# The values of both query halves of a key tile in every second step, in two 512-key attentions

## The chip, the cores and the metric

One core of a Trainium2 chip runs the whole kernel as one launch. The metric is the device time in microseconds (us), the median over runs.

## The reference

The kernel computes a two-layer decoder for 4 sequences of 512 tokens with 128 channels, in fp32. Six blocks follow one another, each added to the residual stream behind a layer norm: an RWKV recurrence, a cross attention to 32 context rows, a feed-forward block that holds a causal attention and a mixture of experts, an attention with relative positions, a latent cross attention, and an attention whose keys are split in two classes. The change concerns the two attentions over 512 keys with 16 heads of 8 channels. Cut to what matters:

```python
# causal, in the feed-forward block ("da" in the kernel)
scores = jnp.einsum('bqhd,bkhd->bhqk', q, k) / np.sqrt(hd)
scores = jnp.where(causal, scores, jnp.finfo(scores.dtype).min)
attn = jax.nn.softmax(scores, axis=-1)
o = jnp.einsum('bhqk,bkhd->bqhd', attn, v).reshape(b, s, d)

# with classes of keys, in the last block ("ga" in the kernel)
l = jnp.where(key_mask[:, None, None, :], logits, -jnp.inf)
a = jax.nn.softmax(l, axis=-1)
return jnp.einsum('bhqk,bkhd->bqhd', a, v)
```

## The kernel before

The blocks run one after the other. Both attentions are built by one function, `attention_stage` (line 508), called as "da" at line 904 (causal) and as "ga" at line 2006 (with classes). Channels lie on partitions. The stage first projects q, k and v and splits q and k into bf16 parts. Then come 16 units, one for each of 4 sequences and 4 groups of four heads (`QUADS`), of eight steps each: 128 steps (`STEPS`). A step covers two heads (`pr`) and one of four tiles of 128 queries or keys.

Each engine has its own instruction queue, whose order is written out by hand; semaphores join them. TensorE's loop (line 742) has 144 iterations. In iteration `step` it issues, in this order:

- `scores(step)` (line 673, matmuls at line 682): queries by keys for two heads, in two of four PSUM banks. VectorE reduces them to row maxima (line 844). A ring of two groups of banks is shared with the turn of the maxima, so that scores wait for what used the slot two places before.
- `scores_t(t)` (line 707, matmuls at 717) with t = step - 13: the transposed scores, keys by queries, less the maxima, in three PSUM banks. They wait until the first of the two exponentials of step t - 1 is done (`exped`). ScalarE turns them into exponentials (`exponentials`, line 783), which lie in three slots of key tiles (`pt`).
- in da only, `mask_scores(step)` (line 693), which adds the causal mask to the scores.
- in every eighth iteration `turn_maxima` (line 702), behind the four small operations of `split_maxima` on VectorE (lines 832 to 838). ScalarE copies the result (line 791), and a DMA puts it beside the queries.
- `values(p)` (line 722, matmuls at 736) with p = step - 16: the exponentials of one key tile times the values, for one half of the queries (`half`), four heads in four column groups of TensorE, added up in one PSUM bank. They wait for the exponentials of the key tile, in da for GpSimd's masking of them (line 643), and at a unit's first for ScalarE's copy of the last unit's output (line 796, `o_out`).

Where the mask leaves a half no queries (`half_of`), `values` does nothing: in da key tiles 2 and 3 have only the second half, and key tile 1 has 128 columns of the first.

Of the kernel before, what the change touches and what calls it, by code (L numbers as in the profile page):

```python
# [504 lines left out]
STEPS = 8 * QUADS  # L505


def attention_stage(nc, g, tag, xn, wq, wk, wv, group, scale, o, causal=False, classes=None):
# [5 lines left out]
    S_LAG, V_LAG = 13, 3  # L514
# [7 lines left out]
    def half_of(kt, half):  # L522
        return max(first_query(kt), half * (T // 2)), (half + 1) * (T // 2)
# [9 lines left out]
    for step in range(STEPS + S_LAG):  # L533
        if step < STEPS:
            ring.append(("scores", step + 1))
        if step % 8 == 1 and 8 < step < STEPS + 8:
            turn_slot[step // 8 - 1] = len(ring)
            ring.append(("maxima", step // 8))
    score_bank = [2 * (n % S_GROUPS) for n, (what, _) in enumerate(ring) if what == "scores"]
    score_slot = [n for n, (what, _) in enumerate(ring) if what == "scores"]  # L540

    with ExitStack() as ctx:
# [9 lines left out]
        with ExitStack() as inner:  # L552
# [21 lines left out]
            with nc.Block() as block:  # L574
# [72 lines left out]
                def _(pe):  # L647
# [25 lines left out]
                    def scores(step):  # L673
                        u, r = divmod(step, 8)
                        pr, qt = divmod(r, 4)
                        if r == 0:
                            pe.wait_ge(stack_loaded[u % NBUF], 16 * LOADS * (u // NBUF + 1))
                        wait_ring(score_slot[step])
                        keys = keys_of(qt)
                        for par in range(2):  # L680
                            rows = slice(64 * par, 64 * par + KS)
                            last = nc.tensor.matmul(g.ps[:, score_bank[step] + par, 0:keys],  # L682
                                                    qst[rows, u % NBUF, pr, bass.ts(qt, 128)],
                                                    kst[rows, u % NBUF, pr, 0:keys], start=True, stop=not causal)
                        if not causal:
                            last.then_inc(scored, 1)

                    def mask_scores(step):
                        qt = step % 4
                        for par in range(2):  # L690
                            bank = score_bank[step] + par
                            for j in range(4):
                                last = nc.tensor.matmul(g.ps[32 * j:32 * j + 32, bank, bass.ts(qt, 128)],  # L693
                                                        g.ident_bf[:, bass.ts(j, 32)], g.lowered_bf[:, :],
                                                        start=False, stop=True)
                        last.then_inc(scored, 1)

                    def turn_maxima(u):
                        pe.wait_ge(split4, u + 1)
                        wait_ring(turn_slot[u])  # L700
                        for qt in range(QT):
                            last = nc.tensor.matmul(g.ps[0:12, 2 * (turn_slot[u] % S_GROUPS), bass.ts(qt, 128)],
                                                    mparts[:, u % 2, qt, :, :, :].rearrange("p a n r -> p (a n r)"),
                                                    g.ident_bf[:, :], start=True, stop=True)
                        last.then_inc(m_turned, 1)

                    def scores_t(t):
                        u, r = divmod(t, 8)
                        kt, pr = divmod(r, 2)
                        if r == 0:  # L710
                            pe.wait_ge(m_loaded[u % 2], 32 * (u // 2 + 1))
                        if t >= 1:
                            pe.wait_ge(exped, 2 * t - 1)
                        q0 = first_query(kt)
                        for par in range(2):
                            rows = slice(64 * par, 64 * par + KT)
                            last = nc.tensor.matmul(g.ps[:, ST_BANK + (2 * t + par) % ST_BANKS, q0:T],  # L717
                                                    kst[rows, u % NBUF, pr, bass.ts(kt, 128)],
                                                    qst[rows, u % NBUF, pr, q0:T], start=True, stop=True)
                        last.then_inc(st_scored, 1)  # L720

                    def values(p):
                        u, r = divmod(p, 8)
                        kt, half = divmod(r, 2)
                        b, quad = divmod(u, 4)
                        lo, hi = half_of(kt, half)
                        if lo >= hi:
                            return
                        if causal:
                            pe.wait_ge(selected, 8 * u + 2 * kt + 2)  # L730
                        else:
                            pe.wait_ge(exped, 2 * (8 * u + 2 * kt + 2))
                        if r == 0 and u >= 1:
                            pe.wait_ge(o_out, u)
                        for j in range(4):
                            last = nc.tensor.matmul(g.ps[32 * j:32 * j + HD + 1, O_BANK, lo:hi],  # L736
                                                    v9[:, QT * b + kt, 4 * quad + j, :],
                                                    pt[:, (4 * u + kt) % SLOTS, j, lo:hi],
                                                    start=r == 0, stop=kt == QT - 1, skip_group_check=True)
                        last.then_inc(pv_done, 1)  # L740

                    for step in range(STEPS + S_LAG + V_LAG):
                        t = step - S_LAG
                        if step < STEPS:
                            scores(step)
                        if 0 <= t < STEPS:
                            scores_t(t)
                        if causal and step < STEPS:
                            mask_scores(step)
                        if step % 8 == 1 and step // 8 - 1 in turn_slot:  # L750
                            turn_maxima(step // 8 - 1)
                        if 0 <= t - V_LAG < STEPS:
                            values(t - V_LAG)

                @block.scalar
                def _(act):
# [1397 lines left out]
```

## Time and profile before

| | us |
|---|---|
| median of 3 runs | 1505.38 (1504.9 to 1508.01) |
| the profiled execution: its time | 1507.97 |
| its span, first to last instruction | 1506.0 |
| TensorE (PE) busy | 1160.2 (77%) |
| VectorE (DVE) busy | 844.8 (56%) |
| ScalarE (ACT) busy | 707.9 (47%) |
| GpSimd (POOL) busy | 306.2 (20%) |
| mean granted TensorE clock | 0.903 of full speed |

Busy times are those of one profiled execution, added up over stages with different limits; each stage has to be read by itself. da's steps lie between about 240 and 403 us of the span, ga's between about 1288 and 1474 us. A row of the timeline gives the start and the length of a run of like instructions; PE rows are matmuls, whose ends are modelled, so that starts tell more than ends. An fp32 matmul stands in the trace as two instructions.

### The profile page before, as it was taken

The numbers are of one execution on the slowest core, as the hardware profiler recorded it, in microseconds if no ns is written. First come the engines' busy times: TensorE is split into PE (matmuls) and PEld (weight loads), VectorE is DVE, ScalarE is ACT, GpSimd is POOL, SyncE is SP. The second block draws the span as 40 slices with busy tenths as digits, with TensorE's granted clock in tenths as the row PEclk, the third lists the DMA queues.
The fourth block names the chain that finished last, engine by engine and source line by source line (L and its number), as shares of the span: only waits on it lengthen the run. The fifth ranks groups of instructions, "written<-read, shape, count | busy, mean of one in ns | idle before, by whom it ended". The sixth has DMA issues, their size and how long they took to land. (4 is left out here: it accounts for less than half of the span.)

```text
span 1506.0 us, 35692 instructions
## 1 busy us (share of the span) xinstructions
PE 1160.2 (77%) x14780; PEld 580.4 (39%) x14780; DVE 844.8 (56%) x1358; ACT 707.9 (47%) x1322; POOL 306.2 (20%) x639
## 2 busy tenths in 40 slices
PE   5677686888748997568999999999666647588884
PEld 2222332333223442246666666666342224122221
DVE  3575336777552223246666666666146234799965
ACT  4101443777522223535565565655232313389891
POOL 1443020333202322033233232222002002000000
PEclk9999866999968999789999999999789878599998
DMA  4000005111005320240030030200200001411100
GB/s 160 1 0 0 1 31 180 47 50 40 2 0 114 68 45 0 73 69 3 4 24 3 5 22 4 15 6 3 15 1 0 1 1 61 156 41 43 38 14 28
DMA packets 133665, 51.61 MB, mean 34 GB/s; under 512 B 103113, under 2 KB 125657, under 8 KB 132858
## 3 DMA queue, kind: packets, MB, share of 16 engines
q1 hardware_dynamic: 133506, 49.34, 14.1%
q8 instruction: 118, 1.93, 0.6%
q14 instruction: 41, 0.34, 0.1%
HBM read 33.12 MB, written 15.81 MB: 32 GB/s over the span
## 5 line engine op out<-in xcount | busy, mean ns | idle before, releaser
L1714 DVE TENSOR_REDUCE re_nmax<-ps 128x1 f32<-128x512 f32 x256 | 158.9, 682 | 113.5 <-PE ps L1548 113.5
L1563 PE MATMUL ps<-const,re_p 128*128 128x128 f32 x1024 | 154.9, 284 | 32.9 <-DVE re_pT L1729 27.0
L1681 ACT ACTIVATE re_p<-ps,re_nmax 128x512 f32<-128x512 f32 x256 | 154.5, 693 | 16.7 <-DVE re_nmax L1714 16.7
L844 DVE TENSOR_REDUCE ga_nmax<-ps 128x2 f32<-128x1024 f32 x128 | 147.7, 1216 | 9.1 <-PE ps L682 9.1
L1670 ACT ACTIVATE re_pT<-ps 128x512 f32<-128x512 f32 x128 | 76.6, 598 | 161.7 <-PE ps L1563 161.7
L783 ACT ACTIVATE ga_pt<-ps 128x512 f32<-128x512 f32 x256 | 139.2, 598 | 20.4 <-PE ps L717 18.6
L1563 PEld LDWEIGHTS ps<-const,re_p 128*128 128x128 f32 x1024 | 109.2, 142 | 63.4 <-ACT re_p L1681 47.1
L844 DVE TENSOR_REDUCE da_nmax<-ps 128x2 f32<-128x256 f32 (+3 forms) x128 | 102.6, 822 | 33.5 <-PE ps L693 32.0
L783 ACT ACTIVATE da_pt<-ps 128x512 f32<-128x512 f32 (+3 forms) x256 | 97.5, 438 | 38.5 <-PE ps L717 37.3
L1729 DVE COPY re_pT<-ps 128x512 f32<-128x512 f32 x128 | 82.5, 685 | 23.2 <-PE ps L1563 22.5
L736 PE MATMUL ps<-ga_pt,ga_v 128*9 128x256 f32 x1024 | 81.4, 386 | 10.3 <-ACT ga_osum L796 10.1
L1069 DVE TENSOR_TENSOR ex_u<-ps,ex_s 128x512 f32<-128x512 f32 x48 | 33.1, 690 | 95.9 <-PE ps L1042 95.9
L163 ACT ACT_TABLE_LOAD x8 | 10.3, 1283 | 152.2 <-PEq L298 92.0
L1538 PE MATMUL ps<-re_keys,re_qbd 32*128 32x512 f32 x512 | 74.8, 655 | 5.5 <-POOL re_qbd L1502 5.5
L643 POOL TENSOR_SCALAR_AFFINE_SELECT da_pt<-da_pt 128x256 f32<-128x256 f32 x128 | 52.7, 412 | 125.4 <-ACT da_pt L783 125.2
L1055 ACT ACTIVATE ex_s<-ps 128x512 f32<-128x512 f32 x48 | 28.7, 597 | 92.8 <-PE ps L1042 92.8
L1511 POOL TENSOR_TENSOR re_qrel<-re_qd,const 128x64 f32<-128x64 f32 x256 | 68.6, 301 | 4.8 <-DMA re_qd<-re_q_scratch 4.8
L1082 POOL TENSOR_TENSOR ex_u<-ex_u,ex_gates 128x512 f32<-128x512 f32 x32 | 40.4, 1264 | 142.7 <-DMA ex_gates<-gates_scratch 73.5
L682 PE MATMUL ps<-ga_kst,ga_qst 50*128 50x512 bf16 x256 | 53.7, 419 | 19.7 <-ACT ga_v L769 10.2
L1498 POOL TENSOR_TENSOR re_keys<-re_k,vec 128x64 f32<-128x64 f32 (+1 forms) x60 | 17.3, 289 | 249.5 <-PE ps L1548 249.5
L1613 PE MATMUL ps<-re_pT,re_v_far 128*9 128x128 f32 x1536 | 65.2, 285 | 0.5 <-ACT re_osum L1690 0.5
L736 PE MATMUL ps<-da_pt,da_v 128*9 128x256 f32 (+1 forms) x768 | 56.2, 362 | 6.3 <-ACT da_osum L796 6.3
(379 smaller groups left out, 2028.6 us busy)
## 6 DMA issues: line engine op xcount, KB each, us to landing
ex_gates<-gates_scratch SPq DMA_DIRECT2D x4, 2048.0 KB, 15.3
da_stacks<-da_qkparts SPq DMA_DIRECT2D x8, 384.0 KB, 3.1
da_qst<-da_stacks SPq DMA_DIRECT2D x32, 96.0 KB, 2.3
da_kst<-da_stacks SPq DMA_DIRECT2D x32, 96.0 KB, 2.3
ga_stacks<-ga_qkparts SPq DMA_DIRECT2D x8, 384.0 KB, 3.1
ga_qst<-ga_stacks SPq DMA_DIRECT2D x32, 96.0 KB
ga_kst<-ga_stacks SPq DMA_DIRECT2D x32, 96.0 KB
da_stacks<-da_qkparts SPq DMA_DIRECT2D x8, 256.0 KB, 3.1
```

Source lines behind the costliest of these rows:

```text
L682: last = nc.tensor.matmul(g.ps[:, score_bank[step] + par, 0:keys], qst[rows, u % NBUF, pr, bass.ts(qt, 128)], kst[rows, u % NBUF, pr, 0:ke ...
L736: last = nc.tensor.matmul(g.ps[32 * j:32 * j + HD + 1, O_BANK, lo:hi], v9[:, QT * b + kt, 4 * quad + j, :], pt[:, (4 * u + kt) % SLOTS, j, ...
L783: nc.scalar.activation(pt[:, (4 * u + kt) % SLOTS, 2 * pr + par, q0:T], g.ps[:, ST_BANK + (2 * t + par) % ST_BANKS, q0:T], ACT.Exp)\
L844: nc.vector.tensor_reduce(nmax[:, u % 2, :, pr, qt], g.ps[:, score_bank[step]:score_bank[step] + 2, 0:keys_of(qt)], AX.X, ALU.max, negate= ...
L1511: nc.gpsimd.tensor_tensor(qrel[:, m, pair, :, :, :, two], qd[:, b % 2, OCT * at:OCT * at + OCT, 4 * pair:4 * pair + 4].unsqueeze(2) .broad ...
L1538: nc.tensor.matmul(g.ps[:, S_BANK + quad, :], qbd[rows, m, :, :, :].rearrange("p o h c -> p (o h c)"), keys[rows, b % 2, m, :], start=True ...
L1563: last = nc.tensor.transpose(g.ps[:, T_BANK + tile % 2, bass.ts(kt, 128)], p[:, QUAD_ORDER[idx], bass.ts(kt, 128)], g.c("ident"))
L1613: last = nc.tensor.matmul(g.ps[32 * j:32 * j + HD + 1, V_BANK, bass.ts(quad, 128)], values, weights, start=kt == 0, stop=kt == QT - 1)
L1670: nc.scalar.activation(pT_of(s, QUAD_ORDER[idx]), turned_of(4 * s + idx), ACT.Identity)\
L1681: nc.scalar.activation(p[:, quad, :], g.ps[:, S_BANK + quad, :], ACT.Exp, bias=nmax[:, s % 2, idx:idx + 1]).then_inc(exped, 1)
L1714: nc.vector.tensor_reduce(nmax[:, s % 2, idx:idx + 1], g.ps[:, S_BANK + quad, :], AX.X, ALU.max, negate=True).then_inc(maxed, 1)
L1729: nc.vector.tensor_copy(pT_of(s, QUAD_ORDER[idx]), turned_of(4 * s + idx))\
```

## The change

Until now `values(p)` came in every iteration from 16 on, one half of the queries each. Now an iteration with an even p issues none, and one with an odd p issues the even half first and then its own. Both belong to the same key tile. The arithmetic stays as it is.

```diff
--- before.py
+++ after.py
@@ -749,8 +749,10 @@
                             mask_scores(step)
                         if step % 8 == 1 and step // 8 - 1 in turn_slot:
                             turn_maxima(step // 8 - 1)
-                        if 0 <= t - V_LAG < STEPS:
-                            values(t - V_LAG)
+                        p = t - V_LAG
+                        if 0 <= p < STEPS and p % 2 == 1:
+                            values(p - 1)
+                            values(p)
 
                 @block.scalar
                 def _(act):
```

## Rows read from the trace of the kernel before

**Rows 1.** Page, costliest groups: busy us, mean ns, idle before, releaser; VectorE's maxima.

```profile
L844 DVE TENSOR_REDUCE ga_nmax<-ps 128x2 f32<-128x1024 f32 x128 | 147.7, 1216 | 9.1 <-PE ps L682 9.1
...
L844 DVE TENSOR_REDUCE da_nmax<-ps 128x2 f32<-128x256 f32 (+3 forms) x128 | 102.6, 822 | 33.5 <-PE ps L693 32.0
```

**Rows 2.** Busy by engine: us; PE, PEld, DVE, ACT, POOL; clock; DMA share; GB/s.

```profile
1311.00:1463.00 152.00, 132.83 (x1436) 37.00 (x1427) 137.26 (x167) 137.21 (x261) 0.00 (x0) 0.99 0.12 35
260.00:390.00 130.00, 112.19 (x2063) 44.48 (x2062) 98.76 (x166) 98.44 (x253) 46.17 (x112) 0.99 0.14 40
```

**Rows 3.** Timeline of PE, ga: start, us, line, tiles, count; one ordinary step.

```profile
1388.69 0.39 PE L682 MATMUL ps<-ga_kst,ga_qst 50*128 50x512 bf16 x2
1388.91 0.38 PE L717 MATMUL ps<-ga_qst,ga_kst 53*128 53x512 bf16 x2
1389.23 0.62 PE L736 MATMUL ps<-ga_pt,ga_v 128*9 128x256 f32 x8
1389.78 0.39 PE L682 MATMUL ps<-ga_kst,ga_qst 50*128 50x512 bf16 x2
```

**Rows 4.** Timeline of ga, all engines: start of one unit and the turn.

```profile
1320.57 0.62 PE L736 MATMUL ps<-ga_pt,ga_v 128*9 128x256 f32 x8 [0.67 <-ACT ga_osum L796]
...
1382.05 1.21 DVE L844 TENSOR_REDUCE ga_nmax<-ps 128x2 f32<-128x1024 f32 x1
...
1383.85 0.62 PE L736 MATMUL ps<-ga_pt,ga_v 128*9 128x256 f32 x8 [0.67 <-ACT ga_osum L796]
...
1384.10 2.35 DVE L844 TENSOR_REDUCE ga_nmax<-ps 128x2 f32<-128x1024 f32 x2
...
1384.63 0.38 PE L717 MATMUL ps<-ga_qst,ga_kst 53*128 53x512 bf16 x2
1385.06 1.09 ACT L783 ACTIVATE ga_pt<-ps 128x512 f32<-128x512 f32 x2 [0.36 <-PE ps L717]
...
1385.47 0.33 PE L702 MATMUL ps<-identb,ga_mparts 128*12 128x128 bf16 x3 [0.45 <-DVE ga_nmax L844]
...
1386.51 0.39 PE L682 MATMUL ps<-ga_kst,ga_qst 50*128 50x512 bf16 x2 [0.23 <-DVE ga_nmax L844]
...
1386.94 6.88 DVE L844 TENSOR_REDUCE ga_nmax<-ps 128x2 f32<-128x1024 f32 x6 [0.49 <-PE ps L682]
```

**Rows 5.** Timeline of PE, tail of ga, where no scores are left.

```profile
1468.98 0.39 PE L717 MATMUL ps<-ga_qst,ga_kst 53*128 53x512 bf16 x2
1469.30 0.62 PE L736 MATMUL ps<-ga_pt,ga_v 128*9 128x256 f32 x8
1470.07 0.39 PE L717 MATMUL ps<-ga_qst,ga_kst 53*128 53x512 bf16 x2
...
1471.47 1.05 PE L736 MATMUL ps<-ga_pt,ga_v 128*9 128x256 f32 x16
```

**Rows 6.** Timeline of da, all engines: one unit from its first values.

```profile
332.43 0.62 PE L736 MATMUL ps<-da_pt,da_v 128*9 128x256 f32 x8 [0.40 <-ACT da_osum L796]
...
333.22 1.13 DVE L844 TENSOR_REDUCE da_nmax<-ps 128x2 f32<-128x256 f32 x2
...
333.79 0.33 PE L702 MATMUL ps<-identb,da_mparts 128*12 128x128 bf16 x3 [0.18 <-DVE da_nmax L844]
...
334.53 0.34 PE L682 MATMUL ps<-da_kst,da_qst 48*128 48x384 bf16 x2
...
335.26 2.42 DVE L844 TENSOR_REDUCE da_nmax<-ps 128x2 f32<-128x768 f32 x3 [0.91 <-PE ps L693]
...
337.41 0.28 PE L682 MATMUL ps<-da_kst,da_qst 48*128 48x256 bf16 x2 [0.50 <-DVE da_nmax L844]
```

**Rows 7.** Timeline of PE at the start of ga, at the lower clock.

```profile
1308.58 1.04 PE L736 MATMUL ps<-ga_pt,ga_v 128*9 128x256 f32 x8
...
1309.55 0.61 PE L682 MATMUL ps<-ga_kst,ga_qst 50*128 50x512 bf16 x2
```

**Rows 8.** Busy by engine, in the relative attention.

```profile
780.00:1080.00 300.00, 265.34 (x6694) 183.96 (x6694) 185.06 (x363) 166.98 (x288) 79.15 (x258) 0.99 0.13 10
```

## The prediction, made before the changed kernel was run

> **What bounds the kernel now.** I read the page first, for which of its groups belong to the two 512-key attentions ("da", the causal one, and "ga", the one with classes), then each stage by itself, then one unit of eight steps in order of time. The page's two groups for line 844 show that VectorE spends 147.7 us on the row maxima in ga with 9.1 us idle before them, and 102.6 us in da with 33.5 us idle, all of it until TensorE delivered [rows 1]. Over a steady stretch of ga, VectorE is busy for 137.26 of 152 us, ScalarE for 137.21 and TensorE for 132.83, all at a granted clock of 0.99; in da TensorE leads with 112.19 of 130 us [rows 2]. So no engine of ga has more than a tenth to spare, and what counts is the order on TensorE's queue.
>
> One ordinary step of ga on that queue is scores, then transposed scores (0.22 us later), then values (0.32 us), then the next scores (0.55 us): 1.09 us from one step's scores to the next one's [rows 3]. VectorE's six reduces in a row take 6.88 us, the last of them 1.22 us, which is a pitch of 1.13 us [rows 4]; this and not TensorE's 1.09 us paces the middle of a unit. Once in a unit VectorE is late for another reason. After the last reduce of a unit come the four small splits, so the next reduce starts 2.05 us after that last one (1382.05 to 1384.10). The turn of the maxima can start only 1.37 us later (1385.47), since it waits for that reduce; the scores behind the turn wait for the next reduce (idle 0.23 us, until 1386.51), and VectorE sits idle for 0.49 us until 1386.94 [rows 4]. The other gap, 0.67 us in which TensorE waits for line 796's copy of the output at 1383.85, delays no reduce: VectorE is at its splits then [rows 4]. From that wait at 1320.57 to the same one at 1383.85 are six units: 10.55 us each [rows 4].
>
> A third chain is hidden just under this one. The transposed scores of a step wait for the first exponential of the step before. In the tail of ga, where no scores are left, transposed scores follow one another at 1468.98 and 1470.07 although the values between them, started at 1469.30, need only 0.55 us of the queue: 1.09 us is the round from transposed scores over ScalarE back to transposed scores [rows 5, 3]. ScalarE starts 0.43 us after they start (1384.63 to 1385.06) [rows 4]. It holds no second step in store, so every delay of transposed scores over 1.09 us is idle time of ScalarE.
>
> **The change part by part.** Nothing is added or removed but the order: the four (eight in the trace, each in two passes) matmuls of an even step p go one iteration later, directly ahead of those of p + 1. Only TensorE's queue changes; no DMA and nothing of SP or POOL moves. The waits move with the matmuls and both halves wait for the same exponentials, which are in by then. The slot of the exponentials comes free with the odd half, whose iteration stays. The wait for line 796's copy goes one iteration later and vanishes. I cost this removal at nothing: it hid under the splits (above). If that cover were not there it would be worth 0.67 us a unit in ga and 0.40 us in da [rows 4, 6].
>
> *The double block.* The tail of ga shows exactly this arrangement: two steps' values one behind the other are 1.05 us from first start to last end, one step's are 0.62 us [rows 5]. The second block costs 0.43 us. So the double block holds the queue for 0.55 + 0.43 = 0.98 us, where two single ones took 1.10. This is less because a block by itself also pays the change of the array's shape: 0.55 is 0.43 and 0.12 more. The Trainium skill, TensorEngine Tiling (Array Packing), section Key Properties, says that a change of tiling mode drains TensorE; the rows agree with the direction, and this rule alone speaks for the change (rival below).
>
> *ga, an ordinary pair.* Put the transposed scores of the long iteration (odd step) at 0. Values start at 0.32, the next scores at 0.32 + 0.98 = 1.30, the short iteration's transposed scores at 1.52. They come 0.43 us too late for ScalarE (1.52 against the round of 1.09). The next long iteration's transposed scores need the short one's first exponential, so they come at 1.52 + 1.09 = 2.61. VectorE needs 2 x 1.13 = 2.26 for the pair and is no longer the bound.
>
> *ga, the pair with the turn.* VectorE can start on the short iteration's scores at 1.30 + 0.43 = 1.73 (the 0.43 from 1386.51 to 1386.94, [rows 4]), on the long one's 1.13 later, at 2.86, which is 0.25 after the long transposed scores at 2.61. At the end of a unit the next unit's first reduce is 2.05 behind that, at 2.30 after those; and the following long iteration starts at 2.61, so this reduce starts at -0.31 of it. The turn comes 1.37 after, at 1.06. From the turn to the next scores TensorE by itself needs 0.74 us with one block of this size (da: 333.79 to 334.53, [rows 6]), so 1.17 with two: scores at 2.23, transposed scores at 2.45, the next long iteration at 2.45 + 1.09 = 3.54.
>
> A unit of ga is then 3 x 2.61 + 3.54 = 11.37 us against 10.55: 0.82 us more. Steps 16 to 127 are 14 such units: 11.5 us. In the tail, 13 steps without scores, a pair takes 0.32 + 0.98 + 1.09 = 2.39 against 2 x 1.09: 0.21 us, six times, 1.3 us. Together 12.8 us.
>
> *da.* With the causal mask only the first two key tiles have queries in the first half, so only two of eight blocks move: the 256-column one of key tile 0, into the iteration with the turn, and a 128-column one of key tile 1. The iteration that the first one leaves has time for it anyway: the turn at 333.79 still waits for the reduce pair that begins at 333.22 behind the splits [rows 6]. The one it joins has none: turn, values, scores at 334.53, then the mask, and VectorE, idle for 0.91 us, starts its reduce at 335.26 [rows 6]. All this comes 0.43 us later. Its three reduces from there run without a gap in 2.42 us, and at 337.41 the scores wait 0.50 us for them, so the shift is handed on to the next unit and no slack takes it up [rows 6]. The 128-column block moves to where those 0.50 us absorb its 0.21 us. So 0.43 x 14 = 6.0 us.
>
> Sum: 12.8 + 6.0 = 18.8 us. The profiled execution has a span of 1506.0 us and took 1507.97, 2.6 us above the median of 1505.38; it would become a span of 1524.8 and a run of 1526.8, and the median 1524.2. I say **1524 us**, 1.2% slower.
>
> **Bounds of the unknown.** The step that no row shows is a double block with scores behind it. Its upper end is two full blocks, 1.10: 0.12 more in four pairs a unit of ga and once a unit in da, 14 x 0.60 = 8.4 us, 1533. The lower end is that ga's pairs are hidden (VectorE's 2.26 us still rules) and da alone pays: 1505.4 + 6.0 = 1511. I take 0.43, since its row has the same two blocks.
>
> **Rivals.**
> *Hidden after all.* ScalarE's 9% of idle time in ga [rows 2] is where slack could come from, if its second exponential and the next step's first could be moved together. Against it stands that the round of 1.09 us goes through the first exponential alone. If it holds for ga only: 1511 us. If da's shift is also taken up (a gap among those three reduces would do it): 1505 us.
> *Faster.* TensorE's queue is the real bound, and each pair saves a change of shape in and one out: 0.12 us behind the values and 0.32 - 0.22 = 0.10 ahead of them, 0.22 us. It decides if the short iteration's transposed scores can come at most 2.26 - 1.09 = 1.17 us after the long one's; they come at 1.52. 56 pairs and the freed waits of 0.67 us would be more than VectorE's whole idle time of 9.1 us, which caps the gain [rows 1]: 1496 us. The skill's rule of the drain, by itself, would give this sign; for it is the busy share of TensorE.
> *The clock.* The double block leaves TensorE idle for some 0.65 us in each pair (2.61 less the 1.96 of queue time). If the granted clock fell to the lower level, as at the start of ga, where the way from values to scores takes 0.97 us and not 0.55 [rows 7], TensorE's part of the pair (2.61 less the 0.66 of 1.09 - 0.43 that is ScalarE's) would become 1.95 x 0.97 / 0.55 = 3.44, and the pair 4.10 us. That is 1.5 us more a pair, 6 us a unit; three such units make 1542 us. Against it: in the relative attention from 780 to 1080 us TensorE was busy for 265.34 of 300 us, with idle time of its own, at a granted clock of 0.99 [rows 8]. For it: the share here falls to about 0.8.
> That the program would not do what it says has no chance worth a line: each engine's order is written out by hand.
>
> **How the numbers follow.** Forecast of 1524 us: 0.81. Clock, about 1542: 0.06. Only da pays, 1511: 0.05. All hidden, 1505: 0.05. Faster, 1496: 0.03. Within 0.2% is about what a measurement of this kernel can tell from no change. Slower by more than that: 0.81 + 0.06 + 0.05 = 0.92; same 0.05; faster 0.03. The range of 1511 to 1535 takes in both bounds and the da-only case and leaves out the clock, the hidden and the faster case, 0.14, and some chance that a term is further off.
>
> **What would show it.** In ga's timeline after: 16 values matmuls in a row over some 1.05 us; transposed scores that alternate between 1.52 and 1.09 us apart; ScalarE idle about 0.4 us once in two steps with TensorE's line 717 as the releaser; VectorE's idle time before line 844 up from 9.1 to over 20 us; a unit of 11.4 us. The wait for the output copy is gone in both stages. In da the reduce behind the turn waits 1.3 us in place of 0.91 and a unit grows by 0.43 us. Wrong would be: pairs of 2.26 us in ga (the third chain is misread), a second block of 0.55 us, or a granted clock well under 0.98 in ga.

## The result: slower by 2.1%, more than forecast

| | us |
|---|---|
| changed kernel, median of 6 runs | 1539.49 (1536.33 to 1548.22) |
| kernel before, median of 6 runs | 1507.61 (1504.9 to 1516.85) |
| ratio | 1.021 (95% interval 1.018 to 1.024) |
| profiled execution after: time, span | 1539.57, 1537.8 |
| forecast | 1524 (1511 to 1535) |

The sign was right. The size was not: 31.8 us more span against a forecast of 18.8. The page's costliest groups after, with busy us, mean ns, idle before and releaser, answer to [rows 1]:

```profile
L846 DVE TENSOR_REDUCE ga_nmax<-ps 128x2 f32<-128x1024 f32 x128 | 150.3, 1219 | 19.5 <-PE ps L682 19.5
L785 ACT ACTIVATE ga_pt<-ps 128x512 f32<-128x512 f32 x256 | 138.8, 595 | 31.8 <-PE ps L717 30.5
...
L846 DVE TENSOR_REDUCE da_nmax<-ps 128x2 f32<-128x256 f32 (+3 forms) x128 | 101.2, 821 | 49.1 <-PE ps L693 47.9
...
L717 PE MATMUL ps<-ga_qst,ga_kst 53*128 53x512 bf16 x256 | 50.6, 391 | 32.7 <-ACT ga_pt L785 32.7
```

VectorE's idle time in ga went from 9.1 to 19.5 us and in da from 33.5 to 49.1, and TensorE now stands for 32.7 us ahead of ga's transposed scores, released by ScalarE. The most useful measure in this document is the length of a unit, from one copy of the output on ScalarE (line 796 before, 798 after) to the next:

| kernel | da: first to last copy, us | ga: first to last copy, us | ordinary unit of da | of ga |
|---|---|---|---|---|
| before | 135.46 | 154.02 | 9.20 | 10.55 |
| changed | 150.31 | 166.64 | 9.63, and six of 11.0 to 11.2 | 11.47 |

The two differences, 14.9 and 12.6, are 27.5 of the 31.8 us. The double blocks begin in a stage's first unit, ahead of its first copy. Counted from a stage's first reduce (239.30 and 1288.26 us before, 240.18 and 1306.59 after) to its last copy, da grew by 15.2 us and ga by 13.7, together 28.9. Of the other 2.9 us, 0.9 come ahead of da's first reduce (it starts anywhere from 236.9 to 242.5 us in the experiments below) and 2.2 between da's last copy and ga's first reduce (885.5 us before, 887.8 after, 885.6 to 894.9 in the experiments, in no order that follows their edits); the end is 0.2 us shorter. These 2.9 us I count as not explained by the change.

In ga TensorE's timeline is what the prediction drew (start, us, line, tiles, count, idle before and releaser). It starts in the iteration with the turn and answers to [rows 3, 4]:

```profile
1363.34 0.39 PE L717 MATMUL ps<-ga_qst,ga_kst 53*128 53x512 bf16 x2 [0.48 <-ACT ga_pt L785]
1364.42 0.33 PE L702 MATMUL ps<-identb,ga_mparts 128*12 128x128 bf16 x3 [0.69 <-DVE ga_nmax L846]
...
1365.60 0.39 PE L682 MATMUL ps<-ga_kst,ga_qst 50*128 50x512 bf16 x2
1365.82 0.38 PE L717 MATMUL ps<-ga_qst,ga_kst 53*128 53x512 bf16 x2
...
1366.90 0.39 PE L717 MATMUL ps<-ga_qst,ga_kst 53*128 53x512 bf16 x2 [0.47 <-ACT ga_pt L785]
1367.22 1.05 PE L736 MATMUL ps<-ga_pt,ga_v 128*9 128x256 f32 x16
1368.20 0.39 PE L682 MATMUL ps<-ga_kst,ga_qst 50*128 50x512 bf16 x2
1368.43 0.38 PE L717 MATMUL ps<-ga_qst,ga_kst 53*128 53x512 bf16 x2
1368.65 0.38 PE L682 MATMUL ps<-ga_kst,ga_qst 50*128 50x512 bf16 x2
1369.59 0.39 PE L717 MATMUL ps<-ga_qst,ga_kst 53*128 53x512 bf16 x2 [0.56 <-ACT ga_pt L785]
1369.91 1.05 PE L736 MATMUL ps<-ga_pt,ga_v 128*9 128x256 f32 x16
...
1372.20 0.39 PE L717 MATMUL ps<-ga_qst,ga_kst 53*128 53x512 bf16 x2 [0.48 <-ACT ga_pt L785]
```

The double block holds the queue from 1367.22 to 1368.20, 0.98 us. The ordinary pair from 1369.59 to 1372.20, from one long iteration's transposed scores to the next one's, is 2.61 us, the pair with the turn 3.56 (forecast 3.54). Only the pair from 1366.90 is off, 2.69 us.

In da, what the prediction had not placed there is seen in the busy time by engine of two neighbouring units (length; PE, PEld, DVE, ACT, POOL; granted clock; DMA share; GB/s), and at their turns:

```profile
309.89:319.52 9.63, 8.12 (x150) 3.57 (x148) 7.00 (x13) 7.03 (x19) 3.31 (x8) 1.00 0.16 44
319.52:330.49 10.97, 9.44 (x150) 4.04 (x148) 7.01 (x13) 7.04 (x20) 3.30 (x8) 0.84 0.13 38
```

```profile
310.65 0.28 PE L682 MATMUL ps<-da_kst,da_qst 48*128 48x256 bf16 x2 [0.41 <-DVE da_nmax L846]
...
312.00 0.33 PE L702 MATMUL ps<-identb,da_mparts 128*12 128x128 bf16 x3 [0.55 <-DVE da_nmax L846]
...
312.22 1.03 PE L736 MATMUL ps<-da_pt,da_v 128*9 128x256 f32 x13
...
320.29 0.28 PE L682 MATMUL ps<-da_kst,da_qst 48*128 48x256 bf16 x2 [0.41 <-DVE da_nmax L846]
...
321.62 0.48 PE L702 MATMUL ps<-identb,da_mparts 128*12 128x128 bf16 x3 [0.55 <-DVE da_nmax L846]
...
322.00 1.91 PE L736 MATMUL ps<-da_pt,da_v 128*9 128x256 f32 x13
```

Both units do the same work. In the first the clock stays at its upper level, and the unit takes 9.63 us. In the second the mean granted clock is 0.84: 0.16 of 10.97 us, twice since the lower level is half of the upper, are some 3.5 us at the lower level. It shows from the turn on, where the same 13 matmuls take 1.91 us in place of 1.03. Read in windows of 0.2 us, each of the changed kernel's six falls in da begins between 0.60 us before the turn and 0.05 us after it.

### The profile page after: what moved, and what is told of

Its sections match the earlier page's. It is cut to its first block and busy times, and to the rows that moved or that the text cites. A ratio compares the mean times of both kernels' runs of the same rounds, so it can differ in the third digit from the quotient of the medians.

```text
span 1537.8 us, 35692 instructions
## 1 busy us (share of the span) xinstructions
PE 1164.6 (76%) x14780; PEld 595.9 (39%) x14780; DVE 846.7 (55%) x1358; ACT 710.2 (46%) x1322; POOL 306.2 (20%) x639
## 5 line engine op out<-in xcount | busy, mean ns | idle before, releaser
L846 DVE TENSOR_REDUCE ga_nmax<-ps 128x2 f32<-128x1024 f32 x128 | 150.3, 1219 | 19.5 <-PE ps L682 19.5
L785 ACT ACTIVATE ga_pt<-ps 128x512 f32<-128x512 f32 x256 | 138.8, 595 | 31.8 <-PE ps L717 30.5
L846 DVE TENSOR_REDUCE da_nmax<-ps 128x2 f32<-128x256 f32 (+3 forms) x128 | 101.2, 821 | 49.1 <-PE ps L693 47.9
L717 PE MATMUL ps<-ga_qst,ga_kst 53*128 53x512 bf16 x256 | 50.6, 391 | 32.7 <-ACT ga_pt L785 32.7
L736 PE MATMUL ps<-ga_pt,ga_v 128*9 128x256 f32 x1024 | 69.2, 384 | 0.2 <-ACT ga_pt L785 0.2
## 6 DMA issues: line engine op xcount, KB each, us to landing
ex_gates<-gates_scratch SPq DMA_DIRECT2D x4, 2048.0 KB, 14.9
```

Source lines behind the costliest of these rows:

```text
L785: nc.scalar.activation(pt[:, (4 * u + kt) % SLOTS, 2 * pr + par, q0:T], g.ps[:, ST_BANK + (2 * t + par) % ST_BANKS, q0:T], ACT.Exp)\
L846: nc.vector.tensor_reduce(nmax[:, u % 2, :, pr, qt], g.ps[:, score_bank[step]:score_bank[step] + 2, 0:keys_of(qt)], AX.X, ALU.max, negate= ...
```

## The experiments

All edits are in `attention_stage`. Two theories are told apart for each stage. For ga, **theory A**: each pair waits for the round from transposed scores over the first exponential back; **rival B**: the load of an engine over the pair counts. For the clock in da, **theory I**: it falls because the moved block leaves TensorE's queue thin ahead of the turn; **theory D**: it falls because of the dense double block behind it. In the expectations of the first four runs "Theory A" stands for what the timelines above say of the stage at hand.

### Each stage alone

```diff
-                        if 0 <= t - V_LAG < STEPS:
-                            values(t - V_LAG)
+                        p = t - V_LAG
+                        late = lambda n: n % 2 == 0 and not causal
+                        if 0 <= p < STEPS:
+                            if p % 2 == 1 and late(p - 1):
+                                values(p - 1)
+                            if not late(p):
+                                values(p)
```

> The change in ga alone; da as before. Theory A (each stage pays by itself, and ga's cost is the round from transposed scores over ScalarE, cut by the double block): ga grows by what it grew in the changed kernel, some 14 us, units of 11.47 us and not 10.55, and the granted clock in ga stays at 1.00; ratio about 1.009. Rival (a stage's time depends on what the earlier one leaves, or ga's growth was partly the clock's phase): ga grows by another amount, under 10 or over 18 us.

Measured: 1526.42 us, ratio 1.0116 (1.0077 to 1.0156). ga's units are 11.47 us, first to last copy 166.64 us as in the changed kernel; da is 135.73 us. So each stage pays by itself, and ga's cost is 12.6 us between its copies (13.7 from its first reduce on).

The same edit with `n % 2 == 0 and causal`:

> The change in da alone; ga as before. Theory A: da grows by some 15 us, of which 5.6 to 6 us are the block that comes 0.43 us later in each unit, and 8 to 9 us are units of 11.0 us in which the granted clock falls to its lower level behind the turn; units of 9.63 us between them; ratio about 1.010. Rival (the fall of the clock was a chance of that run): all units are 9.63 us, da grows by 6 us, ratio 1.004.

Measured: 1527.71 us, ratio 1.0113 (1.0079 to 1.0148). ga is 154.03 us, as before. da is 152.52 us, 17.1 more than before, with units of 9.63 us and seven of 11.0 to 11.3. The fall of the clock was no chance of one run.

### Each of da's two blocks alone

With `n % 8 == 2 and causal` only the 128-column block of key tile 1 moves:

> In da only the 128-column block of key tile 1 (p = 2 in each unit) goes behind, into the iteration of p = 3; key tile 0 and ga stay. Theory A: it joins where VectorE is late anyway, so a unit stays at 9.20 us, the granted clock at 0.99 and the time within 0.1%. Rival (any double block costs its own length, or makes the clock fall): 0.2 us a unit, 3 us, or units of 11 us.

Measured: 1513.78 us, ratio 1.003 (1.0006 to 1.0053). A unit of da is 9.20 us, as forecast, save four of 9.45 to 9.47 (the kernel before has one such) and the last two (9.14 and 7.50 where the kernel before has 8.73 and 6.87); none is near 11 us. da is 137.32 us, 1.9 more than before, but the block itself costs nothing in an ordinary unit. The rest of the 0.3% lies outside the two stages (922.4 us between them against 917.1), where nothing was edited. "Within 0.1%" was a miss for the whole kernel.

With `n % 8 == 0 and causal` only the 256-column block of key tile 0 moves:

> In da only the 256-column block of key tile 0 (p = 0) goes behind, into the iteration with the turn. Theory A: this block alone makes both parts of da's cost: units of 9.63 us where the clock stays, 11.0 us where it falls, da 15 us longer, ratio about 1.010. Rival (both blocks share in it): da grows by clearly less than in the kernel with both, 8 us or so.

Measured: 1526.64 us, ratio 1.0101 (1.0066 to 1.0135); da 148.89 us, units of 9.63 and five of 11.0 to 11.2 us. This block alone makes both parts of da's cost.

### Is it the empty queue or the double block?

The first answer keeps the double blocks and fills the queue where the moved block was:

```diff
-                            for j in range(4):
+                            for n in range(16 if step % 8 == 0 else 4):
+                                j = n % 4
                                 last = nc.tensor.matmul(g.ps[32 * j:32 * j + 32, bank, bass.ts(qt, 128)],
                                                         g.ident_bf[:, bass.ts(j, 32)], g.lowered_bf[:, :],
-                                                        start=False, stop=True)
+                                                        start=False, stop=n >= (12 if step % 8 == 0 else 0))
```

> As the run with the change in da alone, but the mask's eight matmuls of every unit's first step are issued four times (the mask is added again where it already forbids, so the result is the same). They fill some 0.3 of the 0.4 us in which TensorE now waits there for VectorE, the place where the moved block used to be. Theory I (the clock falls because the queue has run thin ahead of the turn): it stays at its upper level, all units are about 9.63 us, da is 8 us shorter than in the run without the filling, ratio 1.005 or so. Theory D (it falls because of the dense double block behind the turn): the falls stay, with units of 11 us in every second place, ratio 1.011.

Measured: 1518.34 us, ratio 1.005 (1.0022 to 1.0077). Two of its units and the stretch from 271 us on, by engine:

```profile
280.24:289.87 9.63, 8.46 (x174) 3.90 (x172) 7.02 (x13) 7.04 (x20) 3.30 (x8) 1.00 0.17 46
289.87:299.50 9.63, 8.46 (x174) 3.91 (x172) 7.01 (x13) 7.03 (x20) 3.30 (x8) 1.00 0.15 44
271.00:400.00 129.00, 112.03 (x2248) 51.41 (x2235) 92.56 (x161) 93.64 (x240) 43.94 (x107) 0.99 0.13 37
```

The same stretch with the change in da alone:

```profile
271.00:400.00 129.00, 110.23 (x1867) 47.18 (x1862) 87.29 (x149) 87.40 (x226) 41.13 (x100) 0.92 0.13 37
```

TensorE does more matmuls, and of the first thirteen units twelve are 9.63 us and one 9.89. Only the next to last is long, 11.31, at a mean granted clock of 0.57; no scores are left there, so there is no mask to repeat. da is 144.35 us in place of 152.52. More work on TensorE made the stage 8.2 us shorter. With the queue filled the double blocks do no harm to the clock in these thirteen units. The filling closes the wait in the unit's first step; the one of 0.55 us ahead of the turn stays:

```profile
299.55 0.63 PE L694 MATMUL ps<-loweredb,identb 128*32 128x128 bf16 x32
300.26 0.28 PE L682 MATMUL ps<-da_kst,da_qst 48*128 48x256 bf16 x2
...
301.60 0.33 PE L703 MATMUL ps<-identb,da_mparts 128*12 128x128 bf16 x3 [0.55 <-DVE da_nmax L850]
```

The second answer takes the moved block away altogether, so that the queue is thin and nothing is joined. This kernel is the one before, and it leaves a part of the causal attention's output out. In da only:

```diff
-        return lo < hi
+        return lo < hi and not (causal and p % 8 == 0)
...
-                        if lo >= hi:
+                        if not has_queries(p):
                             return
...
-                        if r == 0 and u >= 1:
+                        if r == (1 if causal else 0) and u >= 1:
                             pe.wait_ge(o_out, u)
```

> The kernel before with the 256-column values block of key tile 0, first half, left out of da (that part of the causal attention's output is missing). Nothing is joined anywhere; TensorE's queue in the unit's first step is as empty as in the changed kernel. Theory I: the granted clock falls behind the turn in some or every second unit, which makes those units 0.5 to 1.4 us longer than 9.20 although there is less work. Theory D: no double block, so the clock stays at 1.00 and every unit is 9.20 us; no slower than before.

Measured: 1518.65 us, ratio 1.0053 (1.0028 to 1.0077). The first two units:

```profile
267.18:277.69 10.51, 8.94 (x142) 3.40 (x140) 7.11 (x13) 7.04 (x20) 3.31 (x8) 0.84 0.14 41
277.69:286.88 9.19, 7.58 (x142) 3.10 (x140) 7.01 (x13) 7.03 (x19) 3.30 (x8) 1.00 0.17 47
```

Five units are 10.5 to 10.6 us, the others 9.2; da is 141.97 us. Leaving work out made the stage 6.5 us longer than before. The waits ahead of the scores and the turn are 0.41 and 0.55 us again. Theory D is out: the clock falls in a kernel without double blocks and holds in one that has them. Theory I fits both runs. What they do not separate is where in the unit TensorE's work is missing from how much of it is missing. Each clean unit of a kernel without falls keeps TensorE busy for more of its time (7.97 of 9.20 us before, 8.46 of 9.63 filled) than those of the kernels with falls (8.12 of 9.63 changed, 7.58 of 9.20 with the block out). That the falls begin at the turn speaks for the place; the same filling put elsewhere in the unit was not run.

### Which part of ScalarE's work holds ga

Both runs are the one with the change in ga alone, with one of the two exponentials of each step cut to half its columns:

```diff
                         for par in range(2):
+                            end = T // 2 if par == 0 and not causal else T
-                            nc.scalar.activation(pt[:, (4 * u + kt) % SLOTS, 2 * pr + par, q0:T],
+                            nc.scalar.activation(pt[:, (4 * u + kt) % SLOTS, 2 * pr + par, q0:end],
```

> As the run with the change in ga alone, but the first of each step's two exponentials in ga covers 256 of the 512 columns (part of the attention's output is not computed). Theory A (the round from transposed scores over the first exponential back): the round shrinks from 1.09 by about 0.25 us, a unit from 11.47 to about 10.5, where VectorE is the bound again. Rival B (ScalarE's or TensorE's whole load of a pair counts): as much with the second exponential shortened as with the first.

With `par == 1`:

> The counterpart: the second of each step's two exponentials in ga covers 256 of the 512 columns. ScalarE has the same work as in the run with the first one shortened. Theory A: the second exponential lies outside the round, so a unit stays within 0.1 us of 11.47. Rival B: a unit of about 10.5 us as with the first.

Measured: 1516.42 us, ratio 1.0038 (1.0011 to 1.0065), with the first one cut; 1523.93 us, 1.009 (1.0059 to 1.0121), with the second. Transposed scores in TensorE's timeline with the first cut:

```profile
1350.70 0.39 PE L719 MATMUL ps<-ga_qst,ga_kst 53*128 53x512 bf16 x2 [0.33 <-ACT ga_pt L791]
1351.02 1.05 PE L738 MATMUL ps<-ga_pt,ga_v 128*9 128x256 f32 x16
...
1353.09 0.39 PE L719 MATMUL ps<-ga_qst,ga_kst 53*128 53x512 bf16 x2 [0.26 <-ACT ga_pt L791]
```

And with the second cut:

```profile
1354.02 0.39 PE L719 MATMUL ps<-ga_qst,ga_kst 53*128 53x512 bf16 x2 [0.48 <-ACT ga_pt L791]
1354.34 1.05 PE L738 MATMUL ps<-ga_pt,ga_v 128*9 128x256 f32 x16
...
1356.62 0.39 PE L719 MATMUL ps<-ga_qst,ga_kst 53*128 53x512 bf16 x2 [0.48 <-ACT ga_pt L791]
```

The pair is 2.39 us in the first and 2.60 in the second, as long as with both whole. The units are 11.04 and 11.47 us. ScalarE has the same work in both (the slots are set to ones once, at the stage's start, in both), so its load is not the cause; the round through the first exponential is. My number for the unit, 10.5, was a miss: three pairs shrank by 0.21 to 0.22 us each, but the pair with the turn grew from 3.56 to 3.78. There TensorE now waits 1.12 us for VectorE's reduce, and behind the turn the double block still keeps VectorE idle for 0.63 us.

### The order around the turn

In the changed kernel, and in the kernel before, the values are issued ahead of the turn:

```diff
-                        if step % 8 == 1 and step // 8 - 1 in turn_slot:
-                            turn_maxima(step // 8 - 1)
...
+                        if step % 8 == 1 and step // 8 - 1 in turn_slot:
+                            turn_maxima(step // 8 - 1)
```

> The changed kernel, but in the iteration that has both, the double block of values goes ahead of the turn of the maxima and not behind it. Theory I with the sums of the prediction: in da the double block then fills the time in which the queue waits for VectorE anyway, so the block no longer delays the scores (unit back to 9.2 us or a little less), the queue is not empty ahead of the turn, and the granted clock does not fall: da loses its whole 15 us. In ga the three ordinary pairs of 2.61 us stay, so the unit stays between 11.3 and 11.5 us: ratio to the kernel before about 1.009. Rival (the double block itself brings the clock down, or costs its length wherever it stands): da stays 6 us or more above before, ratio 1.013 or more.

Measured for the changed kernel: 1528.47 us, ratio 1.0108 (1.0073 to 1.0143). Of da's units the first thirteen are 9.30 to 9.37 us, none of them with a fall of the clock; da is 138.88 us, 11.4 less than in the changed kernel. ga's units are 11.33 us. The double block is not what costs in da, but where it stands. It fills the wait ahead of the turn, while the one of 0.41 us in the unit's first step stays; the filled kernel has it the other way round. So neither wait alone brought the clock down in da. The unit of 9.34 in place of 9.20 was not foreseen. TensorE's timeline shows the wait that takes the place of the removed one:

```profile
323.66 0.28 PE L682 MATMUL ps<-da_kst,da_qst 48*128 48x256 bf16 x2 [0.41 <-DVE da_nmax L846]
...
324.28 1.04 PE L736 MATMUL ps<-da_pt,da_v 128*9 128x256 f32 x16
325.14 0.39 PE L702 MATMUL ps<-identb,da_mparts 128*12 128x128 bf16 x4
325.51 0.34 PE L682 MATMUL ps<-da_kst,da_qst 48*128 48x384 bf16 x2
...
328.87 0.39 PE L717 MATMUL ps<-da_qst,da_kst 51*128 51x512 bf16 x2 [0.20 <-DMA da_qst<-da_mrows]
```

The later turn makes the DMA of the maxima late for the next unit's first transposed scores.

> The kernel before (single blocks in every step), with only this exchange: values ahead of the turn. The turn waits 0.18 us (da) and 0.45 us (ga) for VectorE there. In da the scores behind the turn should come up to 0.1 to 0.2 us earlier, until the reduce before them holds them: 2 to 3 us less in 15 units. In ga they wait for that reduce already, so the unit stays at 10.55. Ratio 0.998. Rival (the later turn makes the maxima's load late for the next unit's transposed scores): units in ga over 10.6 us, slower than before.

Measured for the kernel before: 1512.53 us, ratio 1.0006 (0.9983 to 1.0029). ga's units stay at 10.55 us, but da's are 9.27 and not 9.1: the scores behind the turn are then held 0.16 us for VectorE, so there was less to gain than I said, and the transposed scores that open a unit start 0.31 us behind their scores in place of 0.12. A miss: 1.0006 is no change that these runs can tell, and no version here beats the kernel before.

## Why the prediction was wrong in size

**What bounds the kernel, and ga: right.** VectorE's pace, the ring at the turn and the hidden round of 1.09 us were read as the traces show them, but for TensorE's share in ga: 132.83 of 152 us leave it an eighth to spare, not less than a tenth. The double block is 0.98 us, the ordinary pair 2.61, the pair with the turn 3.56 against 3.54. The unit is 11.47 against a forecast of 11.37; the 0.10 us is mostly the pair of 2.69. It ends with the transposed scores at 1369.59, which open a unit and wait for the maxima's load as well as for ScalarE. They come 0.94 us behind their scores where the next pair's come 0.86. What that wait costs in itself no run separated. The forecast of 12.8 us for ga counts 14 units and the tail, and stands beside 13.7 us from the first reduce on. Its terms are less close than the sum: the 13 units between copies cost 11.9 us where 13 x 0.82 are 10.7, the first unit's part 1.1, and the tail only 0.7 where 1.3 was forecast. The two shortened exponentials show the cause directly.

**da's shift: right.** Clean units are 9.63 us, which is 9.20 + 0.43, and the reduce behind the turn starts 2.47 us after the reduce pair ahead of it in place of 2.04. (Its idle time is 1.46 and not the 1.3 of the forecast, as that pair now takes 1.02 us in place of 1.13.) The 128-column block is free, as the run with it alone shows.

**The removal costed at nothing: wrong in da.** This is the step that failed. The prediction said that the iteration which key tile 0's block leaves "has time for it anyway", and gave its leaving no term in da's sum, which is the shift of 0.43 us alone. In time on the queue that is so. But there the block was also what kept TensorE busy ahead of the turn. With it gone, the wait ahead of the turn is 0.55 us in place of 0.18, behind one of 0.41 us that stands where the wait of 0.40 us for the output copy was [rows 6], and in six of 15 units the granted clock falls for some 3.5 us and the unit costs 1.3 to 1.6 us more: 8.6 us together. The filled kernel and the one with the block left out show from both sides that the missing work does it. Whether its place or its amount counts, and why the clock then falls, stays open.

**The clock rival: right in kind, wrong in place.** It stood at 0.06, about ga, where the longest idle time per pair was to come. In ga the granted clock stayed at 1.00 in every ordinary unit, though TensorE is busy there for 8.78 of 11.46 us (1339.24 to 1350.70 us); in da it fell with 8.1 of 9.6 us busy. I had not asked the same question of da, because I had put da's change down as a shift by 0.43 us. The row of the relative attention [rows 8] said nothing about either.

**The sum.** 18.8 us of span were forecast, and the two stages show 28.9. ga has 13.7 for 12.8. da has 15.2 for 6.0: 8.6 of the difference are the falls of the clock, the rest is mostly its last two units. The remaining 2.9 us of span lie outside the stages and vary by more between kernels that do not differ there. One thing more is in the time and not in the change: the forecast started from a median of 1505.38 us, and the kernel before came to 1507.61 over 6 runs. With the clock's 8.6 us alone the forecast would have been 1532.8, still inside the range of 1511 to 1535; the base, the parts outside the stages and the small misses make up the rest to 1539.49.

**The other rivals.** "Hidden after all" and "faster" are out: the short iteration's transposed scores come 1.53 us after the long one's (1366.90 to 1368.43), not within 1.17. The double block spares 0.12 us in each (0.98 in place of 1.10), but TensorE was not the bound, so it bought nothing. The Trainium skill's rule that a change of tiling mode drains TensorE (TensorEngine Tiling (Array Packing), section Key Properties) agrees with these 0.12 us, though no run took the change of shape by itself, and by itself it gave the wrong sign as a forecast.

## What to carry to other kernels

When work of an engine is moved, ask what it covered in two senses: what waited behind it, and what the engine does in its old place. In da a block that could leave its place at no cost in queue time cost 8.6 us there through the granted clock, more than the delay where it went (13 x 0.43 = 5.6 us between the copies). And where a consumer holds no step in store, as ScalarE did here, joining two steps' work into one burst delays every second hand-over by the length of the second block, although the total work falls.

## What the runs showed of the hardware that I had not expected

Two gaps of TensorE, 0.41 and 0.55 us within some 1.8 us, go with a fall of the granted clock in about every second unit of da, in a stage where it is busy for 84% of a clean unit (8.12 of 9.63 us). With only one of the two gaps (the filled kernel, and the one with the values ahead of the turn) it fell in none of the first thirteen units. In ga, with 77% busy (8.78 of 11.46 us) and gaps of about 0.5 and 0.7 us spread over the unit, it never fell. So from one stage to another the share of busy time alone does not tell which is at risk. Filling most of the first gap with 24 repeated matmuls of 128 columns a unit removed the falls; leaving out a block of work brought some in. Why every second unit, and not each, was not tested.
